# A Mamba layer and a 16-expert feed-forward layer on one core: computing only the four chosen experts of each token, sorted by expert through DRAM

## What is computed

```python
xb, z = split(rms_norm(x) @ in_proj_w)              # 512 channels each
xc = silu(conv4(xb) + conv_b)
dt, B, C = split(xc @ x_proj_w)                     # 1, 16, 16
dt = softplus(dt @ dt_proj_w + dt_proj_b)
h_t = exp(dt * A) * h_{t-1} + dt * B * xc           # 512 channels x 16 states
y = (sum_s h_t C + D * xc) * silu(z)
return y @ out_proj_w + residual

scores = sigmoid(x @ gate_weight.T)                 # 16 experts in 4 groups
# the two best groups by their two best scores, then the four best experts in them
y = sum over the four of weight * (silu(x @ gate_e.T) * (x @ up_e.T)) @ down_e.T
```

## Time and profile before

| | |
|---|---|
| median of 3 runs | 2791.8 us (2788.87 to 2792.28) |
| span of the profiled execution | 2792.0 us |
| PE busy | 2414.2 us (86%) |
| DVE busy | 2455.6 us (88%) |
| ACT busy | 1628.2 us (58%) |
| POOL busy | 1474.8 us (53%) |
| DMA | 336.65 MB, 121 GB/s over the span |

### The profile page before, as it was taken

The page is one execution under the profiler, slowest core; times in us unless marked ns, Lnnn a source line. Parts: engine busy times, 40 slices in busy tenths (PEclk is TensorE's granted clock), DMA queues, the critical chain, the costliest instruction groups (busy, mean ns, idle before and its releaser), DMA issues.

```text
span 2792.0 us, 27042 instructions
## 1 busy us (share of the span) xinstructions
PE 2414.2 (86%) x8416; PEld 1179.1 (42%) x8416; DVE 2455.6 (88%) x3265; ACT 1628.2 (58%) x3312; POOL 1474.8 (53%) x516
## 2 busy tenths in 40 slices
PE   4556799898989989899998989899898989988898
PEld 1112254443534444354444435354444445444454
DVE  1799998989899998989989898999989899899642
ACT  3566565666666566665666656665666665654331
POOL 0355564646556564655555465565646556565511
PEclk9677899999999999999999999999999999999999
DMA  1532332425244252524435252433525233352221
GB/s 36 226 107 90 129 139 96 160 94 177 77 144 140 98 170 81 188 74 143 133 105 172 79 184 83 136 130 105 179 79 175 95 124 128 100 177 70 64 76 59
DMA packets 164811, 336.65 MB, mean 121 GB/s; under 512 B 15771, under 2 KB 73404, under 8 KB 156220
## 3 DMA queue, kind: packets, MB, share of 16 engines
q1 hardware_dynamic: 164668, 334.93, 35.8%
HBM read 291.35 MB, written 43.52 MB: 120 GB/s over the span
## 4 chain that ended last, share of the span: by engine, by line
PE 42%; DVE 39%; issue 10%; ACT 9%; DMA 0%; SPq 0%; DVEq 0%; ACTq 0%
DVE hs L872 17%; DVE hs L858 9%; PE Gp L416 8%; PE Up L424 7%; PE MY L434 7%; PE FP L343 5%; PE FP L353 4%; PE FP L379 3%; PE Y L446 3%; DVE th L987 3%; DVE th L992 3%; PE FP L361 1%; ACT XC L571 1%; ACT XB L519 1%; ACT DX L636 1%
## 5 line engine op out<-in xcount | busy, mean ns | idle before, releaser
L761 POOL TENSOR_TENSOR hs<-hs,Cb 128x2048 f32<-128x2048 f32 x256 | 1159.1, 4528 | 203.7 <-DVE hs L858 203.7
L501 ACT ACTIVATE dA<-dtr,A 128x512 f32<-128x512 f32 x1024 | 699.7, 689 | 771.3 <-DVE hs L872 768.7
L751 POOL TENSOR_TENSOR th<-th,cmb 128x512 f32<-128x512 f32 x256 | 325.4, 1271 | 1096.8 <-DVE hs L858 980.7
L872 DVE TENSOR_TENSOR_SCAN hs<-dA,carry,hs 128x512 f32<-128x512 f32 x512 | 627.2, 1264 | 31.7 <-ACT dA L501 31.4
L416 PE MATMUL Gp<-x2T,Wgu 128*128 128x512 f32 x1024 | 530.4, 642 | 129.2 <-DVE th L987 129.0
L872 DVE TENSOR_TENSOR_SCAN hs<-dA,hs 128x512 f32<-128x512 f32 x512 | 596.2, 1203 | 50.6 <-ACT dA L501 50.1
L858 DVE TENSOR_TENSOR hs<-dxr,Bb 128x2048 f32<-128x2048 f32 x256 | 586.6, 2292 | 13.4 <-DMA dxr<-dx_d 12.3
L434 PE MATMUL MY<-Wdn,th 128*128 128x256 f32 x2048 | 486.3, 380 | 0.0
L424 PE MATMUL Up<-x2T,Wgu 128*128 128x512 f32 x1024 | 486.2, 597 | 0.0
L434 PEld LDWEIGHTS MY<-Wdn,th 128*128 128x128 f32 x2048 | 383.6, 190 | 136.5 <-issue 84.6
L416 PEld LDWEIGHTS Gp<-x2T,Wgu 128*128 128x128 f32 x1024 | 183.6, 198 | 473.4 <-issue 259.1
(11 more groups left out here) (131 smaller groups left out, 1827.1 us busy)
## 6 DMA issues: line engine op xcount, KB each, us to landing
dtr<-dt_d SPq DMA_DIRECT2D x64, 1024.0 KB, 5.5
dxr<-dx_d SPq DMA_DIRECT2D x128, 512.0 KB, 7.2
cmb<-cm_d SPq DMA_DIRECT2D x256, 256.0 KB, 3.6
Wdn<-in_w_dn SPq DMA_DIRECT2D x256, 128.0 KB, 3.5
dt_d<-XB SPq DMA_DIRECT2D x16, 1024.0 KB, 4.3
dx_d<-DX SPq DMA_DIRECT2D x16, 1024.0 KB, 5.8
Bb<-bc_d SPq DMA_DIRECT2D x64, 256.0 KB, 3.1
Cb<-bc_d SPq DMA_DIRECT2D x64, 256.0 KB, 4.0
```

Source lines behind the costliest of these rows:

```text
L501: act.activation(dA[h % 2][:, :], dtr[:, M % 2, beta, :], ACT.Exp, scale=A[:, k:k + 1]).then_inc(s_dA, 1)
L751: pool.tensor_tensor(th[:, q % NTH, :], th[:, q % NTH, :], cmb[:, q % 2, :], ALU.mult).then_inc(m_a, 1)
L761: pool.tensor_tensor(hs[:, G % NH, :, :], hs[:, G % NH, :, :], Cb[:, s, :].unsqueeze(1).broadcast_to([P, NBETA, CH]), ALU.mult).then_inc(s ...
L872: dve.tensor_tensor_scan(hv, dA[h % 2][:, :], hv, first, ALU.mult, ALU.add).then_inc(s_h, 1)
```

## The change

The experts' part is rebuilt, the spreading of B moves to TensorE, and softplus is made another way.

- Experts. After routing, DVE and PE number the chosen (token, expert) pairs by expert (`p_rank`, `route_ranks`, `set_slots`). Chunks are taken in sets, `LENS`: seven of two chunks and two of one. Each expert's rows begin at a multiple of 128 in a DRAM buffer `xs_d`. POOL writes the normed rows there with indirect DMAs (`scatter`, 16 for each chunk, 128 rows of 1 KB each). The buffer is computed in blocks of 128 rows of one expert, two blocks (a "duo") at a time: `turn` (4 transposes), `gate_up` (8 products of 128 columns), `down` (2 of 256 columns). ACT copies the turned rows and the results out of one PSUM bank `TO` (`take_turned`, `take_down`) and runs `tanh` on 256 columns; DVE's two steps work on 256 columns. The result goes to `ys_d`. The number of blocks is a constant, 16 for each chunk and 16 more for the rounding up: 48 in a set of two chunks and 32 in a set of one, so 200 duos in all. SP reads each block's expert number from DRAM into a register (`value_load`) and loads that expert's 384 KB of weights (`load_wb`); the weights no longer lie in SBUF.
- Return. POOL gathers four rows for each token (`gather`, 16 DMAs for each chunk), ACT makes diagonal matrices of the weights (`z_gains`), and PE sums the four rows with them (`mix`). The last norm now hangs on `MIX_AT`.
- Schedule. By the constants, duos stand in groups 56 to 86, 88 to 118, and so on (three in four groups), 248 to 271 for set 6 without gaps, 272 to 287 and 288 to 303 for the last two. 152 duos stand before group 256, the end of the scans, and 48 behind it. The last `mix` starts at group 308.
- B. `spread_B` is one product of 33 rows and 512 columns for each group; `inputs` reads it from PSUM (`BB`, one bank). `load_B` and `Bb` go.
- Softplus. Abs, Sigmoid, then for each half Square and Ln on ACT; `f_atanh` and `f_delta` on DVE, with one PE product for each quarter. `DX`, dt's store and DX's store move to g 11 and 12; silu of z moves from g 13 to g 14.

```diff
-    def weigh(q):
-        pool.tensor_tensor(th[:, q % NTH, :], th[:, q % NTH, :], cmb[:, q % 2, :], ALU.mult)
+    def scatter(c, n):
+        k, i = SET_OF[c]
+        pool.indirect_dma_start(xs_d[k % NR], bass.IndirectOffsetOnAxis(ap=idx[:, c % 8, n:n + 1], axis=0), x2[:, c % 2, n % TB, :], None).then_inc(st_xs, 16)
+    def gather(c, b, k):
+        pool.indirect_dma_start(gy[:, b % 2, k, :], None, ys_d[kc % NR], bass.IndirectOffsetOnAxis(ap=idx[:, c % 8, m:m + 1], axis=0)).then_inc(ld_gy[b % 2], 16)
...
+    def load_wb(d):
+        if d == D0[k]:
+            sp.wait_ge(st_tab, 16 * (k + 1))
+        if d >= NWB:
+            sp.wait_ge(m_d, d - NWB + 1)
+        for j in range(2):
+            n = k * MOST + 2 * (d - D0[k]) + j
+            e = sp.value_load(tab_d[n:n + 1, 0:1], min_val=0, max_val=NE - 1)
+            sp.dma_start(wb[:, d % NWB, j, :], w_moe[bass.ds(e, 1), :, :].rearrange('o p f -> (o p) f')).then_inc(ld_wb[d % NWB], 16)
...
-    def gate(q):
-    def up(q):
+    def gate_up(d):
+        pe.wait_ge(m_x, d + 1)
+        pe.wait_ge(ld_wb[d % NWB], 32 * (d // NWB + 1))
+        if d >= 1:
+            pe.wait_ge(m_w, d)
+        for u in range(2):
+            for j in range(2):
+                for q in range(KM):
+                    w0 = (2 * q + u) * DE
+                    mm = pe.matmul(GU[:, (2 * u + j) * P:(2 * u + j + 1) * P], wb[:, d % NWB, j, w0:w0 + DE], xgT[:, d % 2, j, q, :], start=q == 0, stop=q == KM - 1)
...
+    def spread_B(G):
+        if G > 0:
+            pe.wait_ge(s_u, G)
+        pe.matmul(BB[:, :], SelB[:, s, :], xd[0:2 * NS + 1, c % 2, :], start=True, stop=True).then_inc(b_full, 1)
...
     def inputs(G):
-        dve.tensor_tensor(hs[:, G % NH, :, :], dxr[:, M % 2, :, :], Bb[:, s, :]...)
+        dve.tensor_tensor(hs[:, G % NH, :, :], dxr[:, M % 2, :, :], BB[:, :]...)
...
-    def f_softplus(p):
-        for m in range(MT):
-            ins = act.activation(dt[:, m, :], FP[:, :], ACT.Softplus, scale=dt_w[:, m:m + 1], bias=dt_b[:, m:m + 1])
+    def f_below(p):
+        for m in range(MT):
+            ins = act.activation(dt[:, m, :], FP[:, :], ACT.Abs, scale=dt_w[:, m:m + 1], bias=dt_b[:, m:m + 1])
+    def f_low(p):
+        act.activation(dt, dt, ACT.Sigmoid, scale=-1.0, bias=neg_ln2)
+    def f_log(p, k):
+        act.activation(x2T[:, :, :], dt[:, 2 * k:2 * k + 2, :], ACT.Square)
+        act.activation(x2T[:, :, :], x2T[:, :, :], ACT.Ln, scale=-ATANH_B, bias=1.0)
...
+    def f_atanh(p, k):
+        dve.scalar_tensor_tensor(out=half, in0=x2T[:, :, :], scalar=-ATANH_0 / ATANH_1, in1=half, op0=ALU.add, op1=ALU.mult)
+    def f_delta(p, m):
+        dve.scalar_tensor_tensor(out=dt[:, m, :], in0=FP[:, :], scalar=0.0, in1=dt[:, m, :], op0=ALU.min, op1=ALU.add)
```

More of the change, by code:

```diff
@@ L677, in _ @@
                 F, R_ = (in_f(p), in_p(p))
-                q = expert_at(G)
                 if 0 <= p < NC:
@@ L681, in _ @@
                     decay(G * NBETA + 3)
+                if G - 3 in DUO_AT:
+                    take_down(DUO_AT[G - 3])
+                if G in DUO_AT:
+                    take_turned(DUO_AT[G])
+                for c_, j in mixing(G):
+                    if j in (4, 6, 8, 10):
+                        z_my(c_, (j - 4) // 2)
+                    if j == 11:
+                        z_squares(c_)
+                    if j in (0, 2, 4, 6):
+                        z_gains(c_, j // 2)
                 if F and g == 1:
@@ L702, in _ @@
                     decay((G + 1) * NBETA + 1)
-                if q is not None:
-                    tanh(q)
+                if G - 1 in DUO_AT:
+                    tanh(DUO_AT[G - 1])
                 if 0 <= p < NC and p % HALVES < HALVES - 1:
```

687 lines of the change are left out of this document (470 added, 217 removed).

## The result

The changed kernel takes 3495.9 us (median of 3 runs, 3490.5 to 3504.0) against 2791.8: 1.2525 times as long, interval 1.250 to 1.255. The profiled execution spans 3488.7 us. The forecast was 3030 us with a range up to 3260. Slower was right, but the forecast had 238 us more and 704 came, about three times as much.

The account below looks back on a forecast made before the run. The prediction took DVE as the bound, with PE near full in middle chunks before the change. Head 94, scans 2577 and tail 360 us gave 3031, stated as 3030 us against 2792.0 before; range 2850 to 3260 us.

Parts of the forecast that it names:

- DVE is the bound in each of them: In chunk 0, chunk 1 and a middle chunk of the kernel before, DVE was taken as the bound.
- 150.7: DVE's own work in a full chunk after the change: 150.7 us, against 154.1 before.
- 15.7 us a chunk: DVE's waits in a full chunk after the change, at g 4, 5 to 7, 10, 14 and the last norm: 15.7 us.
- 0.59 each ... +0.97: ACT's work for a duo: `take_turned` and `take_down` add 0.59 us each, tanh halves, +0.97 us in all.
- fills come some 5 us sooner: g 5 to 7: PE's fills some 5 us sooner, ACT's jobs longer, DVE's wait 4.2 us (before about 5.5).
- no longer a bound: PE loses 18 us of work a chunk and is no longer a bound.
- 4.7 + 3.3 = 8.0 us a chunk: New softplus: 4.7 us of DVE work and a 3.3 us wait at g 10; silu of z at g 14: wait 3.5.
- rival 1: POOL binds: an indirect DMA holds it 2.5 us, 18.5 us a chunk and 22 in the tail, 3275 us; chance 0.17.
- hidden: POOL's scatter groups need 8.1 us, at most 9.3, against 9.6 on DVE, so the indirect DMAs cost nothing.
- 360 forecast: Tail after the scans: 48 duos at 6.3 us (302), routing's chain 15, the end 43: 360 us against 172.5.
- Rival 2: Short tail: register reads nearly free, duos at 4.3 us, ACT's waits stay at 8.4 us a chunk: 2846 us; chance 0.20.
- Rival 3: Faster than before: PE's relief takes DVE's waits away, with the short tail: 2703 us; chance 0.08.

Follow-up runs that it names:

- noexp_oldsoft: Changed kernel without scatters, duos, gathers, mix and last norm (routing stays), and one ScalarE function, Sigmoid, for dt in the softplus's old placement: 2474.9 us.
- a_late: Kernel after with all its results, ACT's copy of the turned rows moved behind the next group's decays and the tanh: 3385.4 us.
- s_noduo: sched with the duos left out; scatters, gathers of zeroed rows, mixing and the last norm stay: 2826.1 us.
- sched: Changed kernel with one Sigmoid for dt, and silu of z, the last three in_proj fills, DX and two stores back at their old groups: 3229.2 us.
- s_late: sched with ACT's copy of the turned rows moved behind the next decays and the tanh; shared bank and mixing stay: 3138.7 us.
- s_nomix_warm: s_nomix with four idle products of 128x512 columns on TensorE at the end of every group: 3478.1 us.
- s_nomix: sched without TensorE's mixing products; ScalarE copies the first of the four gathered rows instead: 3188.9 us.
- nopool: Changed kernel without POOL's 512 indirect DMAs; blocks hold zeros, all else is done: 3379.9 us.
- s_all: sched with short ACT copies and diagonals, weights loaded for the first duos only, no mixing products, an own bank for down products, no indirect DMAs: 2862.9 us.

## Why the prediction was wrong, point by point

**What bounds the kernel.** "DVE is the bound in each of them" held for work: without experts, my steps give 154.1 - 18.9 - 4.9 + 1.0 + 2.35 = 133.7 us of DVE's work a chunk, and noexp_oldsoft shows 133.9 booked and 2.7 us of short pauses, which my figures count as work. With everything I had 150.7; 157.0 and the 2.2 of short pauses that the chunk before had (162.5 - 8.4 - 151.9) make 159.2. The difference is the duos' steps (0.41 us each, not 0.3: 9.7 instead of 7.4) and the held steps, some 6 us a chunk, which I had nowhere.

**The waits are the step that failed.** I had 15.7 us a chunk; it is 196.3 - 159.2 = 37. Of the 466 us that the sum of 3030 lacks, 379 lie in the scans, 65 in the tail and 14 in the head. I priced `take_turned` and `take_down` as "0.59 each ... +0.97", by their length. `take_turned` stands at the head of ACT's group and waits for a product that PE issues in the same group, behind `add_states` and `spread_B`; it costs its 0.60 and, 21 times in two chunks, 1.6 us of standing. Everything in ACT's order behind it inherits that: the jobs A (routing's exponential, the squares of g 4), the next two decays and tanh. I had written that ACT's room in a group is small and then added a step that waits in it, without asking who waits for that. a_late shows this one place at 110 us, 6.8 us of a full chunk; the rows put it on the jobs A and tanh more than on the decays.

The table says which part brings the waits, as a chunk less DVE's busy time: 11.2 us without experts (noexp_oldsoft), 19.1 with moving and mixing (s_noduo), 32.5 with the duos too (sched), 39.3 with the new softplus and its places (after). The last step, 6.8, is what I had for it (3.3 + 3.5). The experts bring the other 21 us, of which moving `take_turned` gives back 10.4 (s_late, 22.1); I had put them at next to nothing (15.7 - 6.8 = 8.9, where the kernel before waits 8.4).

**PE.** The load was near: the sum of the prediction gives 147.8 - 18 = 130 us of work, not the 124 that it goes on with, and at a clock of 0.8 that is 162 us; the rows show 157 at 0.80 and 0.83. "fills come some 5 us sooner" was wrong: DVE waits for PE's fills 4.5 us a chunk, and it waited for none before. "no longer a bound" holds for the load, but not for the order: in the rows of g 9 above, `take_turned` waits because PE has three other products to do before the turn. s_nomix_warm can't price PE's time alone; it shows 59 us of idle work at 23 us a chunk.

**Softplus and places.** I had 4.7 + 3.3 = 8.0 us a chunk and 3.5 for the silu of z; measured 11.9 and 3.5. I had one wait of 3.3 us; the rows show 4.9 a chunk for the logarithm (L1066) and 4.1 for `f_delta`'s fills (L1072), and 2.4 us in which `f_atanh` is held. With the 4.7 of work that is 16.1, more than the 11.9 in all, so a part of it stands where other waits would be. Head: +8 forecast, +23 shown, 18 of it the softplus.

**POOL.** The price of an indirect DMA was right, so rival 1 did not come: 1.2 us taken, and the groups of the page show

```profile
L964 POOL DMA_INDIRECT gy<-ys_d,idx x256 | 251.6, 983 | 378.0 <-ACT gy L683 195.8
...
L950 POOL DMA_INDIRECT xs_d<-x,idx x256 | 264.1, 1032 | 172.6 <-issue 135.1
```

But "hidden" was wrong. I compared POOL's sum with the length of the group and did not ask what runs on DVE at the moment to which `read_out` is pushed. That cost 48 us in the scans and, with the gathers, 63 in the tail.

**The tail.** 360 forecast, 424.7 shown. The volume of the DMAs was right (570 MB forecast, 579.7 on the page). The pace of a duo was near: 6.3 forecast, 6.9 in the median. In this stretch of the tail (SP's issues and PE's products) the term for the registers can be read:

```profile
3300.45 1.66 SPq L335 DMA_DIRECT2D wb<-in_w_moe  x2
...
3306.60 2.02 PE L546 MATMUL GU<-xgT,wb 128*128 128x128 f32 x16 [1.72 <-issue]
...
3308.46 1.89 PE L565 MATMUL MY<-gy,dg 128*128 128x256 f32 x8
```

Two issues with a register read between them span 1.66 us. From one issue to the next it is 1.30 us in the median of the tail's 48 pairs (0.81 to 3.59), so a read with its issue takes 1.3 us, not 1.6. The weights land by some 4.5 us later (4.3 forecast), if it is they for which `gate_up` waits; the row names no releaser. What I left out of the period are the mixing products between duos and the gathers that wait for ACT's squares (POOL stood 115 us for them in the tail): 28 and up to 63 us by s_nomix and nopool. The two can overlap; how they share the 65 us that the tail is longer was not measured. Rival 2, the short tail at 4.3 us a duo, would need all of that gone; s_all gives 3.5. The Trainium skill ("Runtime: NRT & Kernel Launch", Instruction fetch mechanics), cited with some 200 ns for a register, isn't settled by these rows: 1.3 us holds issue and read together.

**The rivals.** Rival 3 needed waits under 5.5 us a chunk; they were 37. Rival 1's total of 3275 us was the nearest to what came, but not by its cause. The range was too narrow upwards since its upper end let "ACT's waits or POOL" be 14 us a chunk longer; the waits alone were 21 longer, and the held steps came on top.

**What stays open.** Of the 15.3 us that moving, mixing and the last norm cost a chunk, 7.4 are DVE's work and some 3 go with the indirect DMAs; where the other 5 go was not tried, nor a `take_turned` that copies a turn of the group before, nor one that is moved behind the jobs A but stays ahead of the decays. What the low clock costs by itself is open too.

## What to carry to other kernels

Price a step that is added to an engine's queue by what it waits for and by what is queued behind it, not by its length: a copy of 0.6 us at the head of ScalarE's group cost 110 us, and moving it behind the group's other jobs, the next decays and tanh gave that back. Then look at which wait has gone: here it was mostly not the one that the theory named. Before work is put on GpSimd, look at which VectorE steps its large products will then run beside: here the scans and the gating steps, which read one input from PSUM, kept their times, and products and small steps in SBUF were held until GpSimd's step ended. Computing three eighths of the rows gained nothing here: in the scans the matrix products were not the bound, and every block adds copies, waits and movement to the engines that are. In counting TensorE's work, count passes: a float32 product has two.
